# Scan blocks of a sixteen-block network on one core: products added up by accumulating transposes, a margin in the planned order of work, streams that begin 12 scan steps apart

## The reference, cut to what matters

```python
for t in range(L):
    A_bar = 1.0 + A * dt[t]                  # block 8: exp(A * dt[t])
    h = A_bar * h + B[t] * dt[t] * x[t]      # one h for each channel and each of 16 states
    y[t] = (C[t] * h).sum(states)
out = ((y + x * D) * silu(z)) @ W_out
```

## Time and profile before

| | us |
|---|---|
| median of 3 runs (lowest, highest) | 3631.7 (3627.91, 3641.34) |
| the profiled execution, its own time | 3608.04 |
| its span, first to last instruction | 3606.7 |
| TensorE busy, VectorE busy, ScalarE busy, GpSimd busy | 3038.5, 2381.2, 2202.3, 1394.7 |
| mean granted TensorE clock | 0.935 of full speed |

### The profile page before, as it was taken

How to read it: one execution, slowest core, us unless ns; L and a number is a source line. 1 busy time by engine, 2 the same in 40 slices (tenths; PEclk the granted TensorE clock), 3 DMA queues, 4 the chain that set the end, 5 groups by cost and what they waited for, 6 DMA issues and landing times. The chain is left out here.

```text
span 3606.7 us, 52771 instructions
## 1 busy us (share of the span) xinstructions
PE 3038.5 (84%) x18500; PEld 1822.3 (51%) x18500; DVE 2381.2 (66%) x6084; ACT 2202.3 (61%) x4827; POOL 1394.7 (39%) x1308
## 2 busy tenths in 40 slices
PE   3678887999889999889999887878788787789987
PEld 0244556657545555444555434546545476554344
DVE  2778774675777776667768889965444444655764
ACT  2456554534466777667767766947656566466874
POOL 1445554444345554224646554643220222100320
PEclk9889998999999999999999999989988999789997
DMA  6343343113200010220101123543532254321420
GB/s 228 97 128 111 105 112 109 57 44 100 68 14 1 1 32 8 76 52 15 51 1 33 33 81 100 166 130 103 135 82 61 61 178 112 99 46 31 92 52 10
DMA packets 216897, 271.96 MB, mean 75 GB/s; under 512 B 39544, under 2 KB 154936, under 8 KB 214584
## 3 DMA queue, kind: packets, MB, share of 16 engines
q1 hardware_dynamic: 192312, 191.11, 18.7%
q0 software_dynamic: 24320, 77.47, 7.2%
HBM read 217.02 MB, written 54.00 MB: 75 GB/s over the span
## 5 line engine op out<-in xcount | busy, mean ns | idle before, releaser
L371 ACT ACTIVATE scratch<-psum 128x512 f32<-128x512 f32 (+6 forms) x1780 | 828.0, 497 | 808.2 <-PE psum L327 578.7
L327 PE MATMUL psum<-scratch 128*128 128x128 f32 (+19 forms) x8016 | 942.9, 324 | 110.2 <-ACT scratch L371 51.0
L463 POOL TENSOR_TENSOR scratch<-scratch 128x512 f32<-128x512 f32 (+3 forms) x536 | 614.7, 1162 | 697.0 <-DVE scratch L424 216.0
L327 PEld LDWEIGHTS psum<-scratch 128*32 128x32 f32 (+9 forms) x8016 | 601.2, 148 | 476.9 <-issue 224.4
L327 PE MATMUL psum<-scratch,w_constants 128*128 128x512 f32 (+2 forms) x848 | 453.5, 635 | 131.8 <-DVE scratch L393 110.2
L371 ACT ACTIVATE scratch<-scratch 128x512 f32<-128x512 f32 (+8 forms) x856 | 395.8, 469 | 246.5 <-DVE scratch L393 167.1
L363 ACT ACT_TABLE_LOAD x357 | 458.0, 1283 | 23.5 <-DVE scratch L393 9.1
L393 DVE TENSOR_TENSOR scratch<-psum,scratch 128x512 f32<-128x512 f32 (+2 forms) x696 | 376.2, 551 | 115.0 <-ACT scratch L371 83.3
L343 PE MATMUL psum<-w_constants,scratch 128*128 128x128 f32 (+2 forms) x1880 | 316.3, 289 | 61.0 <-ACT scratch L371 22.4
L407 DVE TENSOR_TENSOR_SCAN psum<-psum,scratch 128x512 f32<-128x512 f32 x256 | 309.3, 1222 | 77.1 <-ACT psum L371 63.5
L371 ACT ACTIVATE psum<-scratch 128x255 f32<-128x255 f32 (+1 forms) x528 | 221.4, 456 | 193.2 <-DVE scratch L393 188.2
(11 more groups left out here) (108 smaller groups left out, 4016.0 us busy)
## 6 DMA issues: line engine op xcount, KB each, us to landing
scratch<-b_and_c_out SPq DMA_DIRECT2D x256, 256.0 KB
slots_out<-scratch SPq DMA_DIRECT2D x112, 128.0 KB
q_stack<-scratch SPq DMA_DIRECT2D x72, 192.0 KB, 2.4
scratch<-q_out SPq DMA_DIRECT2D x96, 96.0 KB
scratch<-slots_in SPq DMA_DIRECT2D x16, 512.0 KB
q_out<-scratch SPq DMA_DIRECT2D x40, 192.0 KB, 3.1
scratch<-slots_in SPq DMA_DIRECT2D x16, 448.0 KB
scratch<-q_stack SPq DMA_DIRECT2D x24, 288.0 KB
```

Of the source, the lines that this page charges most:

```text
L327: return self.engine.matmul(out, lhsT, rhs, start=start, stop=stop, **kw)
L371: return self.engine.activation(out, src, function, **kw)
L463: return self.engine.tensor_tensor(out, a, b, op)
```

## The change

The scan's products are added differently. In place of the float32 matmul with the identity as stationary operand, the four 128x128 pieces of the product are stationary one after the other and are turned into `self.a` in the transpose mode, adding to what lies there; the bank then holds the sum with tokens on the partitions. After step 15 ScalarE copies it to scratch, four transposes turn it back into `self.a`, and `skip` waits for these. The same helper replaces four 128x128 matmuls with the identity at the end of an `ExpertMix` block.

All `LAG`s but SyncE's are raised by 50 ns, and the rank alone has 100 ns more (`MARGIN`, zero on SyncE), in a method of its own. Filling of TensorE's gaps is planned up to the awaited result plus `LAG`, whatever the rank.

Stream k+1 begins at `cmul` of step 11 of the first sequence of stream k. The weights of `L1_gla` move up by 14 columns of the same buffer.

```diff
 class Engine:
-    LAG = 30
+    LAG, MARGIN = 30, 100
 class Tensor(Engine):
-    LAG, DRAIN, COLD, STEP, SPAN, ENOUGH, WANTED = 55, 160, 50, 13, 3413.3, 0.37, 0.5
+    LAG, DRAIN, COLD, STEP, SPAN, ENOUGH, WANTED = 105, 160, 50, 13, 3413.3, 0.37, 0.5
...
+    def add_turned(self, out, src, ident, start, stop):
+        self.spend(out, src, 109, 1)
+        return self.engine.matmul(out, src, ident, start=start, stop=stop, is_transpose=True)
 class Scalar(Engine):
-    LAG, LN_EXP, LN_EXP_TABLE, SWITCH = 36, (ACT.Ln, ACT.Exp), 6, 1300
+    LAG, LN_EXP, LN_EXP_TABLE, SWITCH = 86, (ACT.Ln, ACT.Exp), 6, 1300
 class Vector(Engine):
-    LAG, DRAIN = 33, 80
+    LAG, DRAIN = 83, 80
 class Pool(Engine):
-    LAG, INDIRECT = 80, 1250
+    LAG, INDIRECT = 130, 1250
 class Sync(Engine):
+    MARGIN = 0
 class Core:
+    def rank(self, p, e):
+        at = self.value[p.key][2] + e.LAG + e.MARGIN if p.key is not None else e.free
+        return max(e.free, at) + e.delay(p.function), at
     def run(self, programs):
...
-                e = self.engines[p.engine]
-                at = self.value[p.key][2] + e.LAG if p.key is not None else e.free
-                rank = max(e.free, at) + e.delay(p.function), at
+                rank = self.rank(p, self.engines[p.engine])
...
-            rank, p = best
-            if p.engine == "pe" and rank[0] > self.engines["pe"].free:
-                self.keep_clock(rank[0], going)
+            p = best[1]
             e = self.engines[p.engine]
+            if p.engine == "pe" and p.key is not None:
+                self.keep_clock(self.value[p.key][2] + e.LAG, going)
 class Scan(Part):
-    D, N, RINGS = 2, 16, 4
+    D, N, RINGS, LEAD = 2, 16, 4, 12
...
+        self.y_token = v2(self.h[2].rearrange("p a b -> p (a b)"), P)
     def pe(self, e):
...
-                e.matmul(self.a, self.c["ident"], self.h[n % 3].rearrange("p a b -> p (a b)"), start=(n == 0),
-                         stop=(n == N - 1)).then_inc(*self.post("acc", bt, n))
+                for i in range(TILES):
+                    chunk, d = divmod(i, D)
+                    last = e.add_turned(self.a[:, i * P:(i + 1) * P], self.h[n % 3][:, d, chunk * P:(chunk + 1) * P], self.c["ident"],
+                                        start=(n == 0 and i == 0), stop=(n == N - 1 and i == TILES - 1))
+                last.then_inc(*self.post("acc", bt, n))
...
             last.then_inc(*self.post("z_in", bt))
+            e.wait_ge(*(yield self["token", "y", bt]))
+            for i in range(TILES):
+                chunk, d = divmod(i, D)
+                last = e.transpose(self.A2[:, d, chunk * P:(chunk + 1) * P], self.y_token[:, i, :], self.c["ident"])
+            last.then_inc(*self.post("turn", "y", bt))
     def act(self, e):
...
             e.wait_ge(*(yield self["acc", bt, N - 1]))
+            e.activation(self.y_token, v2(self.a, P), ACT.Copy).then_inc(*self.post("token", "y", bt))
     def dve(self, e):
...
-            e.wait_ge(*(yield self["acc", bt, N - 1]))
+            e.wait_ge(*(yield self["turn", "y", bt]))
 class ExpertMix(Experts):
...
-            last = e.matmul(self.a[:, t * P:(t + 1) * P], self.by_token[:, 0, t, :], self.c["ident"], start=False, stop=(t == TILES - 1))
+            last = e.add_turned(self.a[:, t * P:(t + 1) * P], self.by_token[:, 0, t, :], self.c["ident"], start=False, stop=(t == TILES - 1))
...
-FROM = {"L1_attn": 3 * SPARE, "L2_scan": 4 * SPARE}
+FROM = {"L1_gla": 2 * SPARE, "L1_attn": 3 * SPARE, "L2_scan": 4 * SPARE}
...
-            ready = (0, "load", "x") if s.index == 0 else parts[s.index - 1][0]["added", 0]
+            ready = (0, "load", "x") if s.index == 0 else parts[s.index - 1][0]["cmul", 0, Scan.LEAD - 1]
```

## The result

| | median us | runs | profiled execution | span | clock |
|---|---|---|---|---|---|
| before | 3632.84 | 3627.91 to 3641.34 (4) | 3608.04 | 3606.7 | 0.935 |
| after | 3608.91 | 3603.64 to 3612.99 (4) | 3610.78 | 3609.5 | 0.910 |

The ratio is 0.9931 (95% interval 0.9907 to 0.9954): 24 us or 0.7% faster. The forecast was 56 us, so 32 us are missing. The two profiled executions do not show the gain, since the one of before lay 24.8 us under its median and the one of after 1.9 us above its own. So I read them for where things lie, not for the difference of their ends.

The account below looks back on a forecast made before the run. No engine bounds the whole: TensorE bounds the middle, VectorE the second scans, and the ramp fills neither. Starts -40, additions -20, way back +4, margin 0 sum to -56 us: 3631.7 to 3576 us, range 3500 to 3655.

Parts of the forecast that it names:

- Starts: Ramp of the first scans: later streams begin sooner, some 6 us lost at each of three hand-overs; -40 us, bounds 0 and 58.
- Additions: Scan products and ExpertMix: transposes cut TensorE's work by about 113 us, a sixth on the path; -20 us, bounds 0 and 60.
- The way back: End of each sequence: ScalarE copy, four transposes and two hand-overs add 1.3 us; +4 us in all, bounds 0 and 21.
- the first rival: Scan stretches: the clock falls because transposes may not keep it up; 84 us more on the path, 3660 us, chance 0.12.
- Margin and lags: Order of all engines: the margin saves at most hand-overs, not long waits; 0, with 52 us either way over 350 waits.
- The second: Order gets worse: ready pieces go before ones a chain waits for, 0.60 us each, 105 us; 3681 us, chance 0.11.
- The third: The ramp's lead is given back as streams meet at TensorE afterwards; 16 of 56 us left, 3616 us, chance 0.16.
- the fourth: Much faster: hand-overs fit throughout (-52) and half the removed TensorE time counts (-40 more); 3484 us, chance 0.13.

Follow-up runs that it names:

- e4: The changed kernel with the four pieces added by ordinary float32 matmuls instead of the transpose mode: ratio 0.9919 to the kernel before, median 3503.68 us.
- e6: The changed kernel itself, unchanged, run again on another chip: ratio 0.9885 to the kernel before, median 3493.13 us.
- e5: The kernel before itself, unchanged, run again on another chip: ratio 1.0000, median 3531.34 us.
- e15: The changed kernel with 3 ns less in every lag but SyncE's: ratio 0.9943 to the kernel before.
- e1: The kernel before with only the transposes of Scan and ExpertMix, the copy and the way back: ratio 1.0389 to the kernel before, median 3670.74 us.
- e7: The changed kernel without the lags, the margin and the filling rule: ratio 0.9983 to the kernel before, median 3525.19 us.
- e9: The changed kernel without the early starts: ratio 1.0099 to the kernel before, median 3655.04 us.
- e10: The kernel before with 3 ns more in every lag but SyncE's: ratio 1.0148 to the kernel before.
- e13: The kernel before with 3 ns less in every lag but SyncE's: ratio 1.0259 to the kernel before.

## Why the prediction was off

**Starts, -40 us: the mechanism held in the ramp, and I sized it too small there.** The second and fourth streams began 22 and 75 us sooner (forecast 18 and 41 at these points), the ramp's scans ended 65 us sooner (forecast 40), and VectorE filled 363.23 of 450 us, 81%. The 6 us that I let go back at each hand-over did not go back. Of its worth at the end, below.

**Additions, -20 us: the work fell, by less.** It fell by 295.3 + 11.1 - 205.7 - 16.9 = 84 us, where my terms make 113. I had worked with the steps from one matmul to the next (0.86 and 0.48 us), while the groups count whole durations, and the clock was lower in the scans than I had put there. What it was worth at the end no pair of runs says: e4 against e6 is 0.3%, 12 us, below the 0.9% by which orders differ.

**The way back, +4 us:** no run separates it.

**The clock, the first rival: present, and cheap.** The clock is lower with the transposes, by the means over twenty traces above. I priced half of the extra time as path, 84 us, which would have made the transposes as a whole 68 us, 1.9%, slower. The comparison over all combinations, below, gives them -0.3% with an error of 0.6%, so nothing like 84 us was on the path. That VectorE is why is argued and not tested: its 98.64 of 102 and 233.12 of 250 us fit that VectorE holds these stretches and TensorE's slower work lies under it. The Trainium skill says in "TensorE: Matmul & The Clock Gate", Part 4, that transposes don't count as TensorE being busy in the same way and that the full clock does not engage for them. These runs agree with its direction (0.84 for 0.92 in the second scans), not with its wording: 24 float32 transposes ran with the clock at 1.00.

**The step that failed: "Margin and lags. ... So I take 0."** I priced these as hand-overs, 350 waits by 0.15 us, with all else in its place. The runs show that little stays in its place: in the traces every edit tried here changes the order of TensorE's work from within the first 300 us on. Ten kernels that differ within their family by 1 to 6 ns spread by 0.9% (one standard deviation, 33 us), and the kernel before is the best of its five: 1.5% (55 us) under their mean. The changed kernel is 0.8% (28 us) under the mean of its own. So the change had first to make up 27 us that its redraw lost, and that is most of the 32 that are missing. My sum had the order at 0; its bounds of 52 us either way hold 27, but for another reason than the hand-overs that they were made of.

Means of families take most of the draw out. They differ by 1.0152 - 1.0008 = 1.4%, 52 us, with a standard error of 0.6% (each 0.9% by the root of 5, the two squared and added): near the 56 us of the forecast, though 0.1 to 2.8% would fit as well, so how near it came is in part luck. The eight combinations of parts give the pieces. With the two means at the ends, the four kernels that have a part against the four that lack it give -1.4% for the starts (forecast -1.1), -0.3% for the transposes (forecast -0.4, the way back in it) and -0.9% for the margin (forecast 0), each with 0.6% of error from the orders. The combinations were not all timed on the same chips, and e6 against the first result shows that this can move a ratio by 0.5%. These are averages over what the other parts are, so they don't add to 1.4. The margin may help; these runs don't show it.

**Rivals 2 to 4.** The second was near the truth in its subject and wrong in its form: no wait of 0.60 us in many places, but another course as a whole, which can go either way. The third, 3616 us, is nearest to the number measured; but the lead was not simply given back in the middle: the second scans began at 2019 instead of 1944 us here, and in the executions of e5 and e6 at 1967 instead of 1920, while the last of them came 59 us sooner there and 18 us sooner here. The range's lower part (the fourth) did not come.

What stays open: which decision in the plan decides between a last stream 16 us behind and one 109 us behind. No version in these runs beats the changed kernel beyond the intervals; e4 (0.9919) and e15 (0.9943) come nearest.

## What to carry to other kernels

Where a planner writes the order of all engines, one build measures the edit and a draw together. Before you believe or drop an edit of such a kernel, shift a constant that means nothing by a few units in both versions, and compare means; here single comparisons ran from -1.2 to +3.9% for parts worth about a per cent. And look at when each stream ends: if one trails, the end is a place to gain that no part of the inner loop reaches.

## What the hardware showed

The same kernel, with the same order of instructions, had medians of 3529 to 3534 us on two chips and 3611 to 3633 on others. Set beside each other, instruction by instruction, the two profiled executions of the kernel before keep their distance in the scans and the middle. They part mainly from about 500 to 950 us (26 us) and from 2500 to 3150 us (59 us), where experts' rows are fetched. There the timeline of the slower execution shows, from one such place:

```profile
2564.81 0.93 PE L327 MATMUL psum<-w_experts,scratch 128*128 128x128 f32 x6
2564.84 0.94 POOL L469 DMA_INDIRECT scratch<-slots_out,scratch  x1 [0.30 <-issue]
...
2567.10 0.56 DVE L393 TENSOR_TENSOR scratch<-scratch,psum 128x384 f32<-128x384 f32 x1 [3.32 <-remote]
...
2570.57 0.28 ACT L371 ACTIVATE scratch<-psum 128x128 f32<-128x128 f32 x1 [5.81 <-remote]
```

and the quicker one (e5) at the same instructions:

```profile
2537.55 0.93 PE L327 MATMUL psum<-w_experts,scratch 128*128 128x128 f32 x6
2537.57 0.94 POOL L469 DMA_INDIRECT scratch<-slots_out,scratch  x1 [0.30 <-issue]
2537.74 0.56 DVE L393 TENSOR_TENSOR scratch<-scratch,psum 128x384 f32<-128x384 f32 x1 [1.23 <-PE psum L327]
...
2538.52 0.28 ACT L371 ACTIVATE scratch<-psum 128x128 f32<-128x128 f32 x1 [1.02 <-PE psum L327]
```

The matmuls are as long and GpSimd issues its gathers as fast, but ScalarE starts 4.8 us after the end of the last matmul instead of 0.04. The waits of the kernel before on the slower chip, total us, times, longest, list them under a releaser that the profile can't name:

```profile
ACT scratch L371 <- remote: 81.7, 24, 7.6
DVE scratch L393 <- remote: 53.3, 14, 9.2
```

e5 has no such row. Neither have e1, e4, e6 and e7, from the two quicker chips, while the changed kernel, e9, e10 and e13, from slower ones, all have them. The changed kernel gained 24 us, by medians, on the first chip and 36 on that of e5 and e6. That a release comes late while GpSimd issues gathers back to back fits this, but no run here tried it; the cause stays open.
